# A graph network layer pair: four source tiles loaded row by row in place of two, and 411 gathers in place of 413

## The reference

```python
def layer0(h, src, dst, etype, norm):
    hsrc = h[src]                                  # one row of x per edge
    coef = w_comp[etype]                           # 8 coefficients per edge
    msg = sum(hsrc @ weight[b] * coef[:, b][:, None] for b in range(8)) * norm
    return relu(segment_sum(msg, dst) + bias)

def layer1(h, edge_attr, src, dst):
    neigh = segment_sum(h[src] + edge_attr, dst)
    rst = (1 + eps) * h + neigh
    y = batchnorm(rst @ W1 + b1) * gamma + beta
    return relu(y) @ W2 + b2

x1  = layernorm(x  + layer0(x, src, dst, edge_type, edge_weight))
out = layernorm(x1 + layer1(x1, edge_attr, src, dst))
```

## Time and profile before

| | |
|---|---|
| time, median of 3 runs (lowest to highest) | 592.95 us (591.94 to 595.67) |
| time of the profiled execution | 591.92 us |
| its span in the profile | 590.1 us |
| mean granted TensorE clock | 0.909 |
| PE, PEld, DVE busy | 85%, 72%, 79% of the span |
| ACT, POOL busy | 37%, 68% of the span |

### The profile page before, as it was taken

One profiled execution on the slowest core, in us unless ns is written; L12 is line 12 of the kernel. 1 busy time (PEld: TensorE's weight loads), 2 busy tenths in 40 slices (PEclk: granted clock), 3 DMA queues, 4 the chain that ended last, 5 costly groups with the idle time before them and its releaser, 6 DMA issues. The chain is left out here.

```text
span 590.1 us, 13829 instructions
## 1 busy us (share of the span) xinstructions
PE 499.6 (85%) x3981; PEld 422.8 (72%) x3981; DVE 464.3 (79%) x1835; ACT 220.3 (37%) x325; POOL 399.0 (68%) x431
## 2 busy tenths in 40 slices
PE   3679887997977977878986888988999797798995
PEld 2458787876866766757575676677989787797675
DVE  5999999989998699989789888895554655655476
ACT  8914446445343264434354442430000000003386
POOL 7777777777777777777777777777777777750000
PEclk9987779597687898989889999999999978989999
DMA  5423757565676395667675775887575765743003
GB/s 142 126 51 90 249 186 220 174 200 180 201 242 238 87 308 161 217 216 245 206 228 189 227 258 189 269 278 226 182 243 141 230 197 154 227 121 119 2 1 109
DMA packets 103807, 108.18 MB, mean 183 GB/s; under 512 B 11726, under 2 KB 90822, under 8 KB 103730
## 3 DMA queue, kind: packets, MB, share of 16 engines
q1 hardware_dynamic: 84286, 77.88, 40.5%
q0 software_dynamic: 13216, 27.09, 17.1%
q10 hardware_dynamic: 6228, 2.30, 1.5%
HBM read 81.67 MB, written 25.56 MB: 182 GB/s over the span
## 5 line engine op out<-in xcount | busy, mean ns | idle before, releaser
L921 POOL DMA_INDIRECT gathered_flat<-in_x_dram,src_i x399 | 382.8, 959 | 121.6 <-issue 89.3
L1016 ACT ACTIVATE adj_flat<-psum 128x500 f16<-128x500 f32 (+1 forms) x208 | 127.4, 612 | 193.1 <-PE psum L1302 185.4
L1278 PE MATMUL psum<-weighted,gathered_flat 128*128 128x96 f32 (+1 forms) x804 | 142.8, 305 | 27.1 <-DMA gathered_flat<-in_x_dram,src_i 27.0
L1271 PEld LDWEIGHTS psum<-hot,attrs 128*128 128x128 f32 x832 | 146.5, 214 | 12.4 <-issue 9.7
L1278 PEld LDWEIGHTS psum<-weighted,gathered_flat 128*128 128x128 f32 x804 | 122.3, 213 | 30.9 <-DMA gathered_flat<-in_x_dram,src_i 30.7
L1782 DVE TENSOR_SCALAR etype_hot<-iota_key,key_t 128x300 f16<-128x300 f16 (+1 forms) x416 | 135.3, 327 | 0.0
L1271 PE MATMUL psum<-hot,attrs 128*128 128x12 f32 (+1 forms) x832 | 132.4, 236 | 2.4 <-DVE weighted L1663 2.4
L1302 PE MATMUL psum<-etype_hot 128*128 128x300 f16 (+1 forms) x416 | 128.0, 345 | 3.4 <-DVE etype_hot L1782 3.3
L1779 DVE TENSOR_SCALAR etype_hot<-iota_key,gathered_flat 128x128 f16<-128x128 f16 x416 | 106.8, 257 | 15.2 <-issue 8.7
L1911 DVE TENSOR_TENSOR sums_flat<-psum,sums_flat 128x180 f32 x208 | 71.2, 342 | 26.1 <-DVE sums_flat L1859 4.8
L1859 DVE TENSOR_TENSOR sums_flat<-psum,sums_flat 128x132 f32 x160 | 45.8, 293 | 52.6 <-PE psum L1374 23.5
(11 more groups left out here) (168 smaller groups left out, 390.2 us busy)
## 6 DMA issues: line engine op xcount, KB each, us to landing
attrs<-in_edge_attr_dram SPq DMA_DIRECT2D x51, 512.0 KB
adjacency<-adj_flat SPq DMA_DIRECT2D x26, 900.0 KB
coef<-adjacency SPq DMA_DIRECT2D x24, 288.0 KB, 4.7
gathered_flat<-in_x_dram,src_i POOLq DMA_INDIRECT x399
sums_flat<-adjacency SPq DMA_DIRECT2D x10, 576.0 KB
sums_flat<-adjacency SPq DMA_DIRECT2D x10, 288.0 KB
sums_flat<-adjacency SPq DMA_DIRECT2D x6, 360.0 KB, 5.8
sums_flat<-in_x_dram SPq DMA_DIRECT2D x128, 0.5 KB
```

Of the source, the lines that this page charges most:

```text
L921: pool.indirect_dma_start(gathered_tile(t), None, x[:, :], bass.IndirectOffsetOnAxis((src_slots if t < AHEAD else src_i)[:, t:t + 1], 0)). ...
L1016: nc.scalar.activation(window, counts, ACT.Copy).then_inc(counts_copied, 1)
L1271: product = nc.tensor.matmul(last_row(u, i), attrs[:, s * GROUP + j, :], hot_tiles(s, i)[:, u % GU, :], start=(u % 2 == 0 and i == 0), sto ...
L1278: nc.tensor.matmul(unit_psum(u)[:, 0:B, STARTS[i]:STARTS[i] + WIDTHS[i]], gathered_tile(u * UNIT + i), weighted_tiles(u // GU % 2, i)[:, u ...
```

## The change

Gathers stop at tile 410 (SCALARED = T - 5 = 411). Tiles 411 and 412 are loaded row by row by ACT, five rows per u from u = 152 to u = 203 (51 times five and once one). Tiles 413 and 414 are loaded row by row by SP, ten rows per step from step 23 to step 48. The rows land in parts of the sums that are no longer used. PE waits for tile 411 at unit 205, for 412 and 413 at unit 206, for 414 at unit 207, each by a semaphore of its own. SP's wait after the loop is for the gathers of unit 205 instead of 206. In front of each of SP's block loads of a step stands a new wait (`pace`): from step 38 on, the i-th load of step g waits until PE has read unit 4(g - 1) + i.

```diff
-ROWS_EACH = 5
+ROWS_EACH = 10
 SCALAR_UNIT = 152
-SCALAR_EACH = 3
+SCALAR_EACH = 5
...
-    ROWED = T - 2
+    ROWED, SCALARED = T - 3, T - 5
...
-        row_place, row_sources = sums[:, 0, 0:F], sums[0:1, 0, F:2 * F].bitcast(I32)
-
-        scalar_place, scalar_sources = sums[:, 0, 2 * F:3 * F], sums[0:1, 0, 3 * F:4 * F].bitcast(I32)
+        def dead_sums(k, at, n):
+
+            return sums[:, 0, PARTS[k][0] + at * F:PARTS[k][0] + (at + n) * F]
+        row_sources, scalar_sources = (dead_sums(k, 2, 2)[0:1, :].bitcast(I32) for k in range(2))
 
         def gathered_tile(t):
 
             if ROWED <= t < T - 1:
-                return row_place
-            if t == ROWED - 1:
-                return scalar_place
+                return dead_sums(0, t - ROWED, 1)
+            if SCALARED <= t < ROWED:
+                return dead_sums(1, t - SCALARED, 1)
...
-                def load_rows_of_tile(first, last):
+                def load_rows_of_tiles(first, last):
                     sp.wait_ge(rows_in, 16 * 6)
...
-                    for i, row in enumerate(rows):
-                        sp.dma_start(row_place[first + i:first + i + 1, :],
-                                     x[bass.ds(row, 1), :]).then_inc(rows_in, 16)
+                    for i, row in enumerate(rows, first):
+                        sp.dma_start(gathered_tile(ROWED + i // P)[i % P:i % P + 1, :],
+                                     x[bass.ds(row, 1), :]).then_inc((rows_in, src_in)[i // P], 16)
+
+                def pace(g, i):
+                    if 2 * g >= ALL_COUNTED and i < GU:
+                        sp.wait_ge(tiles_read, ((g - 1) * GU + i + 1) * UNIT)
...
-                    for n in range(NRUNS):
-                        if RUNS[n][5] == g:
-                            load_run(n)
+                    own = [n for n in range(NRUNS) if RUNS[n][5] == g]
+                    for i, n in enumerate(own):
+                        pace(g, i)
+                        load_run(n)
                     if 0 <= g - EARLY_STEP < EARLY_LOADS:
+                        pace(g, len(own))
                         load_last(LOAD_ORDER[g - EARLY_STEP])
                     if g == ROW_STEP:
                         load_row_sources()
-                    if 0 <= (g - ROW_STEP - 1) * ROWS_EACH < P:
+                    if 0 <= (g - ROW_STEP - 1) * ROWS_EACH < 2 * P:
...
-                sp.wait_ge(gather_in[(U - 2) % RU], landed(U - 2))
+                sp.wait_ge(gather_in[(U - 3) % RU], landed(U - 3))
...
-                    if t + 1 >= ROWED:
+                    if t >= SCALARED:
                         continue
...
-                for i, row in enumerate(rows):
-                    act.dma_start(scalar_place[first + i:first + i + 1, :],
-                                  x[bass.ds(row, 1), :]).then_inc(etype_rows_in, 16)
+                for i, row in enumerate(rows, first):
+                    act.dma_start(gathered_tile(SCALARED + i // P)[i % P:i % P + 1, :],
+                                  x[bass.ds(row, 1), :]).then_inc((etype_rows_in, norm_in)[i // P], 16)
...
-                    if 0 <= (u - SCALAR_UNIT) * SCALAR_EACH < P:
+                    if 0 <= (u - SCALAR_UNIT) * SCALAR_EACH < 2 * P:
                         at = (u - SCALAR_UNIT) * SCALAR_EACH
-                        load_scalar_rows(at, min(P, at + SCALAR_EACH))
+                        load_scalar_rows(at, min(2 * P, at + SCALAR_EACH))
...
-                    if u * UNIT < ROWED:
+                    if u * UNIT < SCALARED:
                         pe.wait_ge(gather_in[u % RU], landed(u))
-                    else:
+                    if u == U - 3:
+                        pe.wait_ge(etype_rows_in, 16 * (5 + P))
+                    if u == U - 2:
+                        pe.wait_ge(norm_in, 16 * (4 + P))
                         pe.wait_ge(rows_in, 16 * (6 + P + FRESH))
-                    if (u + 1) * UNIT == ROWED:
-                        pe.wait_ge(etype_rows_in, 16 * (5 + P))
+                    if u == U - 1:
+                        pe.wait_ge(src_in, 16 * (4 + P))
```

More of the change, by code:

```diff
@@ L114, in gnn_resnorm_kernel @@
     TWINS = 3
-    ROWED = T - 2
-    assert ROWED * P + P + FRESH == E and ROWED % UNIT == 0
+    ROWED, SCALARED = T - 3, T - 5
+    assert (T - 1) * P + FRESH == E and (SCALARED - 1) % UNIT == 0
     COUNT_FASTER = 2 * RING * GROUP
@@ L677, in landed @@
         def landed(u):
-            return (u // RU + 1) * 16 * UNIT - (16 if (u + 1) * UNIT == ROWED else 0)
+            return (u // RU + 1) * 16 * UNIT - (16 if (u + 1) * UNIT - 1 == SCALARED else 0)
         def tiles_of(n):
@@ L800, in load_row_sources @@
                     sp.wait_ge(st_var, PART_AT[2])
-                    sp.dma_start(row_sources, src[ROWED * P:ROWED * P + P].rearrange("(t e) -> t e", t=1)).then_inc(rows_in, 16)
-                def load_rows_of_tile(first, last):
+                    sp.dma_start(row_sources, src[ROWED * P:(ROWED + 2) * P].rearrange("(t e) -> t e", t=1)).then_inc(rows_in, 16)
+                def load_rows_of_tiles(first, last):
                     sp.wait_ge(rows_in, 16 * 6)
@@ L826, in _ @@
                         load_row_sources()
-                    if 0 <= (g - ROW_STEP - 1) * ROWS_EACH < P:
+                    if 0 <= (g - ROW_STEP - 1) * ROWS_EACH < 2 * P:
                         at = (g - ROW_STEP - 1) * ROWS_EACH
-                        load_rows_of_tile(at, min(P, at + ROWS_EACH))
+                        load_rows_of_tiles(at, min(2 * P, at + ROWS_EACH))
                     if g == GROUPS - 3:
@@ L1061, in load_scalar_sources @@
             def load_scalar_sources():
-                first = (ROWED - 1) * P
-                act.dma_start(scalar_sources, src[first:first + P].rearrange("(t e) -> t e", t=1)).then_inc(etype_rows_in, 16)
+                act.dma_start(scalar_sources, src[SCALARED * P:(SCALARED + 2) * P]
+                              .rearrange("(t e) -> t e", t=1)).then_inc(etype_rows_in, 16)
             def load_scalar_rows(first, last):
```

## The result

| | before | after |
|---|---|---|
| median of the runs (lowest to highest) | 593.87 us (591.94 to 595.67, 4 runs) | 644.15 us (643.14 to 644.26, 4 runs) |
| profiled execution | 591.92 us | 644.16 us |
| its span | 590.1 us | 642.5 us |
| mean granted TensorE clock | 0.909 | 0.874 |

The ratio of after to before is 1.0833, 95% interval 1.0792 to 1.0874: slower by 50 us. The forecast was 633 us with a range of 617 to 656.

What follows compares the result with a forecast made beforehand. Before, POOL's gathers, PE and DVE meet at the end; after, ACT's queue decides. Profiled 591.9 + 37.7 (ACT's rows) + 2.5 (cold clock) - 0.3 (fewer gathers) = 631.8 us; median 1.0 us above, so 633, range 617 to 656.

Steps and rivals of the forecast that it cites:

- ACT's queue decides: ACT's row loads from 397.19 us on end late, so PE's unit 206 comes 37.7 us later.
- rival A: ACT's queue finishes its sets in time and the gathers decide: 589.4 to 592 us, not slower; chance 5%.
- The set of five: ACT's register reads and row issues: a period of 3.25 us a set, against 2.48 us for three rows.
- The stations: ACT's work queued behind rows, parts 4 to 6, late at 418.7 to 530 us; PE's and DVE's loss inside 37.7 us.
- rival C: PE and DVE lose more than ACT, which then waits for them: 5 to 15 us added, 638 to 648; chance 15%.
- The gate: PE's last long wait is ahead of unit 206, for the last row of tile 412, there at 567.0 us.
- The landing of a row: The last row of tile 412, issued by ACT at 564.0 us, lands 3.0 us later.
- The cold restart: After PE's wait, units 206, 207 and sixteen L1348 run at low clock: 2.5 us more, between 0 and 4.
- The gain of 0.3 us for two gathers less: POOL's gather stream ends 2.5 us earlier; taken alone, units 205 and 206 gain 0.3 us, between 0 and 2.5.
- SP's rows and the new waits at nothing: SP's five more rows per step cost nothing, at most 1.8 us in few steps; block-load waits are already passed.
- Rival B: Every part of ACT's set grows with the rows, 4.13 us a set: 44 us on top, 677 us; chance 8%.

Runs made afterwards that it cites:

- ACT's part alone: Kernel before with ACT's tiles 412 and 413 in sets of five, SP one tile, no new waits, 412 gathers: 644.54 us, ratio 1.0851.
- the run with the stations first: Changed kernel with ACT's row set issued behind its other work of the same u instead of ahead of it: 647.19 us, ratio 1.0855.

## Why the prediction was right, and where its sum was short

The time lies inside the range, 11 us above the forecast, and on the side forecast. Step by step:

- **ACT's queue decides: right.** ACT's part alone makes the whole loss, the rest without it none. The 256 rows kept ACT's queue from 394.74 to 576.74 us, 0.71 us each with their register reads. The Trainium skill's sentence that starting a transfer is "usually small relative to the DMA itself" (DMA: Bandwidth & Descriptors, Issuing engines are not separate DMA queues) was cited beside rival A. For one row this case does not speak against it, 0.71 us beside 2.8 us from the end of its issue to its use; but the starts of one queue follow one another, and their sum decided.
- **The set of five: the term that was mis-sized.** I took 1.23 us for reading the registers and starting as a constant and added only two rows, 3.25 us. Over the fifty sets to the last full one the period is (573.50 - 394.74 - 1.1) / 50 = 3.55 us, with the prediction's 1.1 us for the two loads of x. 50 x 0.30 is 15.2 us too little; the first row went out 2.45 us earlier than before, which leaves 12.7 us, and 560.8 + 12.7 is the 573.5 us at which that set starts. The rows themselves were sized right (2.02 us against 2.0); the read was not: 0.98 us for three numbers in before, on the mean 0.25 x 0.81 + 0.75 x 1.39 = 1.25 us for five, 0.27 us a set. Part of it was to be had from before: the two gaps ahead of SP's rows that I took for bounds hold a read of 1.26 us (step 45) and one of 0.71 us (step 47), the second from a multiple of four. Three sets in four are of the dear kind, so SP's mean for five is about 0.25 x 0.70 + 0.75 x 1.25 = 1.11 us, and 1.11 - 0.98 = 0.13 us more a set would have forecast some 640 us. That ACT's fives cost another 0.14 us more than SP's, no row of before showed.
- **The stations: right in kind, late by the same term.** Forecast 418.7, 428.5, 448.7 (the sum as written gives 448.5) and 530 us; measured 419.69, 430.08, 452.08 and 540.18. PE and DVE were held at them, and ACT waited for neither, so rival C's extra 5 to 15 us did not come.
- **The gate: one wait was missed.** The prediction had PE's last long wait at unit 206 for the last row. PE's first L1358 asks for the last station of part 6 ahead of that, which in before was met in time, and PE waited there 8.20 us. By my reckoning it cost nothing beyond the sum, as the row would have held unit 206 at nearly the same time: issued by 573.50 + 3.24 = 576.74, and with the 2.8 us of the run with the stations first there at 579.5, where unit 206 was multiplied at 579.84 us. Both gates end the same queue. That the wrong gate cost the forecast nothing more is luck: the two lie some 0.3 us apart here.
- **The landing of a row:** 3.0 us assumed, 2.8 us measured from the end of the issue to the use, 3.3 us from its start. The Trainium skill's 2.0 us of fixed cost (DMA: Bandwidth & Descriptors, Anatomy of one DMA — SWDGE (gpsimd) path), weighed beside it, lies further off here; its place is the path of GpSimd, and these rows were issued by ACT.
- **The cold restart:** 2.5 us forecast, 1.2 of it for units 206 and 207. Those ran at full speed (0.68 us for four products at 579.84 us); the first L1358 stood between the wait and them. The second L1358 takes 1.6 us more than before and stays in the tail (59.6 against 57.9 us), though PE had waited only 1.38 us just ahead of it and 1.16 us in before, where the clock stayed at 1.00; why it fell here is open. The first takes 1.8 us more, of which no run tells how much the last row would have hidden. So the size is near by luck: 1.9 us from unit 206 to the end.
- **The gain of 0.3 us for two gathers less:** not there. With unit 206 later by 12.8 us than forecast (50.5 against 37.7), a restart shorter by 0.6 and no gain, the profiled execution lies 12.4 us above the 631.8. The median lies 11 us above the forecast, as it lay 1.0 us above the profiled execution in the runs known ahead and does not in after. Why the first row went out 2.45 us earlier than before, no run isolates.
- **SP's rows and the new waits at nothing: right.** Ten rows took 4.02 us and SP still waited for PE at its attribute loads (268.3 us in 46 steps); with and without the waits the ratios agree within their intervals.
- **Rival B** was half right in its reason: the read does grow. But the gap did not grow in proportion to the rows (1.23 to 1.51 us from three to five, where rival B had 2.05), and 677 us was far off.

What stays open is why the first number's place decides what a read of four or more costs; the runs show that it does and how much.

## What to carry to other kernels

A queue that reads registers and issues small transfers is an engine of its own: it has no busy share, and its price per item (here a read of about a microsecond for each set, 0.385 us for each further row) has to be set against the pace of the loop that it runs beside. Of such a read look for its own line, on any engine that has one with the same count, before taking what lies between two transfers as a constant; and if it takes four numbers or more, begin it at a multiple of four. Before work is moved to a queue with little slack, list everything that stands behind it in that queue and who waits for it: the wait that ended last here was for a station with which the change had nothing to do.

## What the runs showed of the hardware that was not expected

- A read of four or more registers from the on-chip memory costs by where its first number lies: five numbers on ACT take 0.81 us from a multiple of four and 1.39 us from one behind it; four take 0.58 and, from two behind, 1.18 us; ten on SP 1.16 and 2.26 us. Five always reach into a second group of four, so it is the beginning that decides and not the crossing. Three take 0.98 us wherever they begin.
- Fewer gathers gave nothing that could be measured: with 412 the ratio to before was 0.9968 and, once more, 1.0014; with 411 and ACT nearly in time (PE waited 2.6 us for it) 1.0016.
